# Mamba, token norm, shared expert and routing as one static program, with buffers laid over each other

## The chip, the cores and the metric

The kernel runs on one core of one Trainium2 chip. The metric is the device time in microseconds of one execution, as a median over runs. Smaller is better. All arithmetic is in float32, but for the one-hot tables of the routing (float16).

## What is computed

One layer of a network on an input of 2 sequences of 1024 tokens with 512 features: a Mamba block, then a mixture of experts, each on a layer-normed copy of its input and each with two residuals.

```python
x = L0_attn_x                                   # (2, 1024, 512)
x = x + _L0_attn_ref(_layernorm(x), ...)        # Mamba: D_INNER 1024, 16 states, conv of 4 taps
x = x + _L0_ffn_ref(_layernorm(x), ...)
# in _L0_ffn_ref, T = 2048, H = 512, E = 32 experts of I = 256, K = 4, shared expert of 512:
flat = (x * rsqrt(mean(x**2) + eps) * norm_w).reshape(-1, H)
scores = softmax(flat @ router_w.T)
topk_w, topk_ids = top_k(scores, 4);  topk_w = topk_w / sum(topk_w)
routed = sum over the token's 4 experts of topk_w * (silu(g) * u) @ w2[e],  g, u = split(flat @ w1[e])
shared = (silu(flat @ sg) * (flat @ su)) @ sd
out = x + routed + shared
```

## The kernel before, in words

The program is a sequence of blocks. At the end of a block all engines meet. A block has one stream of instructions for each engine, and semaphores between them. The blocks are `constants`, `mamba`, `tokens`, `routing` and `experts`.

`mamba` is fully unrolled. It goes over 4 segments of 512 tokens (two for each sequence) and in each over 8 channel blocks of 128, so 32 steps g. In a step ScalarE makes the decays (L500), VectorE spreads delta times x over the states (L646) and runs 16 scans (L656), GpSimd multiplies the states by C (L753), and TensorE sums them into `y_ps` (L846) with identity matmuls. Between these sums TensorE does other small pieces, the gap items: the input projection of the next segment ("in"), its delta and B/C projections ("dtr", "bc"), the gate ("z"), the transposes of the normed input ("turn"), and the output projection of the segment before ("out"). They share two PSUM banks (`work`) in turn, by a table `where` that is written out ahead. B and C of a segment go through a DRAM tensor `bcd` and come back replicated to all partitions (`b_rep`, `c_rep`). The last segment's output projection has no step left to hide in: its 4 tiles are the list `closing`. The result x1 is written to DRAM.

`tokens` reads x1 back in 4 groups of 4 tiles of 128 tokens, in loops (`Fori`) on every engine. VectorE and ScalarE make the layer norm and the RMS norm (`norm_steps`), with the weight `norm_w` multiplied in, and the rows `flat` are stored to DRAM for the experts' gathers. For each tile TensorE transposes `flat` (`transposes`, L1091), multiplies by the router, the gate and the up weights (`gate_up`, L1099, L1106), transposes the activation between gate and up of the next tile (`act_transposes`, L1116), and multiplies down (`down`, L1123). VectorE adds the result to `c.base`, which SP stores to the output. The norm of group r+1 stands among the work of group r. The weights, and the first four experts' weights (`w1_ring`, `w2_ring`), are loaded at the start of this block.

`routing` makes from the logits of all 16 tiles the list of tokens for each expert tile: softmax, the four largest, one-hot masks, ranks by matmuls with triangular and one matrices (L1343 to L1345), tile tables, and the list itself from one-hot matmuls (L1355). Nearly all is a chain of small VectorE instructions, each of which waits for the one before (`Chain.settle`).

`experts` goes over the tiles of 128 slots, sorted by expert, two at a time. GpSimd gathers rows of `flat` by an indirect DMA (L1441), TensorE transposes them (L1559), multiplies by w1 (L1573), transposes the activation (L1584), multiplies by w2 (L1591), VectorE scales the rows (L1542), and GpSimd adds them to the output in DRAM by a second indirect DMA (L1456). SP loads the weights of expert e+4 when expert e is done.

## Time and profile before

| what | us |
| --- | --- |
| median of 3 runs | 1881.86 (1879.46 to 1888.6) |
| the profiled execution | 1884.71 |
| its span | 1883.0 |
| TensorE busy | 1613.8 (86%) |
| VectorE busy | 1205.5 (64%) |
| GpSimd busy | 1128.1 (60%) |
| ScalarE busy | 790.8 (42%) |

Times in the profile count from the start of the span. PE is TensorE and PEld its weight loads, DVE is VectorE, ACT ScalarE, POOL GpSimd, SP the engine that issues the plain DMAs. A float32 matmul stands as two records in the trace, so 4 of them are "x8". "128*32" is a matmul whose weights have 32 columns. PEclk is the granted clock of TensorE as a share of 2.4 GHz. In the program's order: Mamba's scan lasts until about 1020, the last output projection until about 1052, tokens until 1277, routing until 1339, and experts to the end.

### The profile page before, as it was taken

Reading aid. Unit: us, or ns where it says so; the run is one execution under the profiler, and the core shown is the slowest. Engines: PE = TensorE matmul, PEld = TensorE weight load, DVE = VectorE, ACT = ScalarE, POOL = GpSimd, SP = SyncE. Lnnn points to the kernel's source line nnn. Section 1 sums busy time; section 2 is a strip of 40 time slices with the busy share of each in tenths; the row PEclk is TensorE's granted clock in tenths of the full one; section 3 lists DMA queues with packets and bytes.
Section 4 is the critical chain, followed back from the end, with each engine's and each line's share of the span. In section 5 each row is a group of like instructions: output and inputs, shape, how many; then the busy total and the mean of one; then the engine's idle time right before and its main releaser. Section 6 shows DMA issues by size and latency. Waiting matters only on the chain. (4 is left out here: it accounts for less than half of the span.)

```text
span 1883.0 us, 18250 instructions
## 1 busy us (share of the span) xinstructions
PE 1613.8 (86%) x4198; PEld 726.3 (39%) x4199; DVE 1205.5 (64%) x1707; ACT 790.8 (42%) x1287; POOL 1128.1 (60%) x695
## 2 busy tenths in 40 slices
PE   5679998999988999898779599992599999999995
PEld 2233433444333444333333254551244444444442
DVE  3599999999999999899994233317532333333331
ACT  4466576665766666566562243410011111111110
POOL 0199899998889988999985111100144444544443
PEclk9889999999999999999999799996699999999998
DMA  3600125101151110410000621210167676676663
GB/s 111 264 18 23 38 65 200 35 33 39 54 209 37 31 36 26 181 43 25 7 17 12 246 85 61 67 39 17 33 150 214 176 198 187 173 196 185 155 145 57
DMA packets 65360, 182.86 MB, mean 97 GB/s; under 512 B 10016, under 2 KB 14368, under 8 KB 56608
## 3 DMA queue, kind: packets, MB, share of 16 engines
q1 hardware_dynamic: 47232, 138.48, 20.8%
q0 software_dynamic: 18080, 43.82, 11.9%
q8 instruction: 20, 0.33, 0.1%
q14 instruction: 28, 0.23, 0.0%
HBM read 147.65 MB, written 34.62 MB: 97 GB/s over the span
## 5 line engine op out<-in xcount | busy, mean ns | idle before, releaser
L753 POOL TENSOR_TENSOR h<-h,c_rep 128x2048 f32<-128x2048 f32 x128 | 579.0, 4527 | 29.9 <-DVE h L656 24.9
L846 PE MATMUL bank<-h,ident 128*128 128x512 f32 x916 | 444.7, 628 | 88.9 <-POOL h L753 68.7
L500 ACT ACTIVATE bank<-delta,a_neg 128x512 f32<-128x512 f32 x512 | 335.8, 681 | 167.2 <-DVE h L656 166.5
L846 PEld LDWEIGHTS bank<-h,ident 128*128 128x128 f32 x916 | 178.3, 199 | 332.6 <-issue 212.9
L656 DVE TENSOR_TENSOR_SCAN h<-bank,state,h 128x512 f32<-128x512 f32 x256 | 305.9, 1259 | 0.5 <-ACT bank L500 0.5
L656 DVE TENSOR_TENSOR_SCAN h<-bank,h 128x512 f32<-128x512 f32 x256 | 290.6, 1199 | 1.4 <-ACT bank L500 1.4
L1573 PE MATMUL h_ps<-w_ring,xT 128*128 x640 | 285.4, 599 | 3.5 <-issue 3.4
L646 DVE TENSOR_TENSOR h<-bank,b_rep 128x2048 f32<-128x2048 f32 (+1 forms) x105 | 227.4, 2184 | 45.1 <-ACT bank L493 31.3
L1524 DVE TENSOR_TENSOR act<-gs,h_ps 128x256 f32<-128x256 f32 x80 | 33.7, 421 | 248.4 <-ACT gs L1497 248.4
L1497 ACT ACTIVATE gs<-h_ps 128x256 f32<-128x256 f32 x80 | 30.7, 384 | 379.6 <-PE h_ps L1573 379.6
L1573 PEld LDWEIGHTS h_ps<-w_ring,xT 128*128 128x128 f32 x640 | 120.8, 191 | 163.3 <-issue 163.3
L1591 PE MATMUL y_ps<-w_ring,aT 128*128 x320 | 149.5, 610 | 11.9 <-ACT aT L1501 11.9
L1456 POOL DMA_INDIRECT out<-y,into x80 | 128.0, 1601 | 30.5 <-issue 26.6
L1440 POOL TENSOR_TENSOR held<-ones 128x1 f32<-128x1 f32 x82 | 22.9, 279 | 191.2 <-DVE which L1534 129.0
L740 POOL TENSOR_TENSOR h<-du,b_rep 128x2048 f32<-128x2048 f32 (+1 forms) x32 | 125.3, 3916 | 12.3 <-PE bank L846 12.3
L806 PE MATMUL bank<-xnT,w_in 128*128 128x512 f32 x256 | 119.8, 615 | 12.2 <-ACT zs L467 10.4
L830 PE MATMUL bank<-xnT,w_res 128*128 128x512 f32 x256 | 119.9, 612 | 0.0
L820 PE MATMUL bank<-w_out,xs 128*128 128x512 f32 x256 | 114.8, 593 | 0.0
L1075 POOL TENSOR_TENSOR base<-x_group,xl_group 128x512 f32 x16 | 22.0, 1406 | 127.8 <-DVE xl_group L1026 127.8
L1441 POOL DMA_INDIRECT xg<-flat,which x82 | 83.3, 1016 | 24.4 <-POOL held L1440 12.3
L1455 POOL TENSOR_TENSOR sent<-ones 128x1 f32<-128x1 f32 x80 | 29.8, 373 | 101.2 <-DMA out<-y,into 88.5
L1591 PEld LDWEIGHTS y_ps<-w_ring,aT 128*128 128x128 f32 x320 | 58.1, 191 | 79.8 <-issue 79.8
(214 smaller groups left out, 1835.9 us busy)
## 6 DMA issues: line engine op xcount, KB each, us to landing
w_ring<-in_w SPq DMA_DIRECT2D x32, 1024.0 KB, 6.2
b_rep<-bcd SPq DMA_DIRECT2D x16, 1024.0 KB, 6.9
c_rep<-bcd SPq DMA_DIRECT2D x16, 1024.0 KB, 4.9
w_ring<-in_w SPq DMA_DIRECT2D x32, 512.0 KB, 8.4
w_in<-in_w_in_x SPq DMA_DIRECT2D x32, 256.0 KB, 2.6
w_res<-in_w_in_res SPq DMA_DIRECT2D x32, 256.0 KB, 2.7
xa<-in_x SPq DMA_DIRECT2D x20, 256.0 KB, 3.0
xb<-in_x SPq DMA_DIRECT2D x16, 256.0 KB, 2.7
```

The lines of the kernel that those rows point to most:

```text
L500: eng.activation(da[j][:], delta[:, g % 2], ACT.Exp, scale=a_neg[:, col:col + 1])\
L646: eng.tensor_tensor(h[:, q, a:b], du_ps[:].unsqueeze(1).to_broadcast([P, b - a, SEG]), b_rep[:, Q * q + a:Q * q + b, :], ALU.mult).then_in ...
L656: eng.tensor_tensor_scan(h[:, q, j, :], da[j][:], h[:, q, j, :], init, ALU.mult, ALU.add)\
L740: eng.tensor_tensor(h[:, q, a:b], du[:].unsqueeze(1).to_broadcast([P, b - a, SEG]), b_rep[:, Q * q + a:Q * q + b, :], ALU.mult).then_inc(S ...
L753: ins = eng.tensor_tensor(h[:, q], h[:, q], c_rep[:, Q * q:Q * q + Q, :], ALU.mult)
L806: ins = eng.matmul(out[:], w_in[:, n % 2, k, :], xnT[:, s % 2, k, :], start=(k == 0), stop=(k == KC - 1))
L820: eng.matmul(out[:], xs[:, s % 2, d, i * P:(i + 1) * P], w_out[:, d, :], start=(d == 0), stop=False)
L830: ins = eng.matmul(out[:], w_res[:, i % 2, k, :], xnT[:, s % 2, k, :], start=(k == 0), stop=(k == KC - 1))
L846: ins = eng.matmul(y_ps[:], c.ident[:], h[:, q, j, :], start=False, stop=(q == NQ - 1 and j == Q - 1))
L1456: eng.indirect_dma_start(out=dram.out_rows, out_offset=bass.IndirectOffsetOnAxis(ap=into[:, u:u + 1], axis=0), in_=y[:, u, :], in_offset=N ...
L1573: ins = eng.matmul(h_ps[i][:], xT[:, i, k, :], c.w1r[:, bass.ds(ring[i], 1), k, :].rearrange("p a n -> p (a n)"), start=(k == 0), stop=(k ...
L1591: ins = eng.matmul(y_ps[i][:], aT[:, i, k, :], c.w2r[:, bass.ds(ring[i], 1), k, :].rearrange("p a n -> p (a n)"), start=(k == 0), stop=(k ...
```

## The change

1. `mamba`, `tokens` and `routing` become one block, `front`, without loops. Its buffers have fixed addresses (`Memory`): `new` takes fresh space, `over` lays a tensor over one that is no longer needed. `c.base` lies over `h`, the shared weights over `xnT` and `w_in`, `flat_T` over `b_rep`, the expert ring over `c_rep` and `w_out`, all tables of the routing over `xs`.
2. The first 12 tiles of x1 are loaded into `c.base` as each quarter of `h` has been summed for the last time. The last 4 tiles never go to DRAM. The norm is made as in Mamba: statistics on VectorE, Ln and Exp on ScalarE, small products on GpSimd, and then one ScalarE instruction a tile for `flat` and one for `base`.
3. `norm_w` is no longer in `flat`. It is multiplied in behind the transposes: `flat_turned` in `front`, `rows_out` in `experts`, both on VectorE.
4. `closing` holds TensorE's whole order from the last output projection to the last down matmul.
5. The routing is cut into nine steps, which VectorE does behind `add(i)` of the shared expert's tiles 0 to 8. TensorE's matmuls for it stand behind `dn(i)`.
6. The B/C projection writes four column groups of 32 partitions, 128 tokens each, in place of one output of 32 x 512. `bcd` is written by four DMAs.
7. The blank rows are stored near the start of Mamba, behind the first `b_rep` and `c_rep` loads, and SP waits for them. Two more small loads stand at the start. The first four gathers are issued at the end of `front`.

```diff
-def mamba(nc, c, dram):
+def front(nc, c, dram):
+        c.base = over("base", "h", [P, TT, DM])
+        w_g, w_u = over("w_sg", "xnT", [P, KC, SH]), over("w_su", "xnT", [P, KC, SH], skip=KC * SH * 4)
+        flT = over("flat_T", "b_rep", [P, TT, KC, P])
...
-        closing = [("out", NSEG - 1, i, half) for i in range(ST) for half in (0, 1)]
+            items = [last(0, 0), last(0, 1), last(1, 0), ft(0), last(1, 1), ft(1), last(2, 0), ft(2), lg(0), last(2, 1),
+                     ft(3), lg(1), last(3, 0), ft(4), lg(2), ft(5), last(3, 1), ft(6), lg(3), ft(7)]
+            for t in range(4, 8):
+                items += [lg(t), ft(t + 4)]
+            items += [lg(t) for t in range(8, 12)]
+            items += [gu(0), ft(12), ft(13), lg(12), ft(14), lg(13), ft(15), lg(14), lg(15)]
+            for i in range(TT):
+                items += ([gu(i + 1)] if i + 1 < TT else []) + [at(i), dn(i), rt(i)]
...
                 def write_bc(s):
                     read(eng, "bc", s, 0)
-                    eng.dma_start(dram.bcd[s], bc[:]).then_inc(S["bcd_written"], 16)
+                    for t in range(ST):
+                        eng.dma_start(dram.bcd[s, :, t * P:(t + 1) * P], bc[2 * NS * t:2 * NS * (t + 1), :])\
+                            .then_inc(S["bcd_written"], 16)
...
+                eng.wait_ge(F["blank_made"], 1)
+                eng.dma_start(dram.flat[T:T + P, :], blank[:]).then_inc(F["blank_stored"], 16)
+                eng.dma_start(dram.out[TT], blank[:, 0:DM]).then_inc(F["blank_stored"], 16)
+                eng.wait_ge(F["blank_stored"], 32)
                 eng.dma_start(w_out[:], dram.w_out).then_inc(S["out_loaded"], 16)
...
+                def load_x1(q):
+                    eng.wait_ge(S["y_summed"], LAST * NQ + q + 1)
+                    for u in range(2):
+                        eng.wait_ge(x1_stored[u], 16 * (q + 1) * ST // 2)
+                    eng.dma_start(c.base[:, q * ST:(q + 1) * ST, :], dram.x1_seg[q]).then_inc(f_loaded[q], 16)
...
+                last_out(0)
+                for t in range(4):
+                    flat_row(t)
+                flat_var(1)
+                flat_root(1)
+                for t in range(4, 8):
+                    flat_row(t)
+                flat_var(2)
+                flat_root(2)
+                residual(NSEG - 1, 2)
+                last_out(1)
+                flat_row(8)
+                residual(NSEG - 1, 3)
+                flat_row(9)
+                last_out(2)
...
+                for i in range(TT):
+                    if i + 1 < TT:
+                        silu_gate(i + 1)
+                    act_turned(i)
+                    if i < 8:
+                        base_row(8 + i)
...
+                for t in range(6, TT):
+                    flat_turned(t)
+                route_scores()
+                mult(0)
+                route_ids()
+                for i in range(TT):
+                    if i + 1 < TT:
+                        mult(i + 1)
+                    add(i)
+                    route(i)
...
+                            for t in range(ST):
+                                ins = eng.matmul(out[2 * NS * t:2 * NS * (t + 1), 0:P], w_xp[:, d, DR:],
+                                                 xs[:, s % 2, d, t * P:(t + 1) * P], start=(d == 0), stop=(d == DC - 1))
...
-                    eng.tensor_scalar(xT[:, i], xT_ps[i][:].rearrange("p (k t) -> p k t", k=KC), 0.0, None, ALU.add)\
-                        .then_inc(S["xT_ready"], 1)
+                    eng.tensor_tensor(xT[:, i], xT_ps[i][:].rearrange("p (k t) -> p k t", k=KC),
+                                      c.norm_f[:].unsqueeze(2).to_broadcast([P, KC, P]), ALU.mult).then_inc(S["xT_ready"], 1)
```

The route steps in order: `route_mask` (tile 0), `route_counts`, `route_places`, `route_tables`, four times `route_hot` for four tiles of tokens, and `route_list` (tile 8). `ft(t)` transposes tile t of `flat`, `lg(t)` multiplies by the router, `gu(i)` by gate and up, `at(i)` transposes the activation, `dn(i)` multiplies down, `rt(i)` is TensorE's part of the routing.

## Rows read from the trace of the kernel before

**Rows 1.** The page, part 1: busy us, share, instructions of each engine.
```profile
PE 1613.8 (86%) x4198; PEld 726.3 (39%) x4199; DVE 1205.5 (64%) x1707; ACT 790.8 (42%) x1287; POOL 1128.1 (60%) x695
```

**Rows 2.** Windows by stage: length, busy us (instructions), PE clock, DMA share, GB/s.
```profile
1020.00:1052.00 32.00, 31.07 (x73) 13.49 (x71) 0.69 (x1) 4.49 (x7) 0.00 (x0) 1.00 0.13 42
1052.00:1080.00 28.00, 6.71 (x20) 4.79 (x21) 10.46 (x19) 7.37 (x16) 6.02 (x5) 0.58 0.91 345
1127.00:1177.00 50.00, 48.74 (x160) 25.05 (x160) 15.37 (x29) 20.55 (x33) 5.50 (x4) 1.00 0.18 63
1277.00:1312.00 35.00, 4.73 (x10) 2.09 (x10) 29.66 (x132) 1.91 (x2) 0.41 (x3) 0.57 0.07 15
1312.00:1339.00 27.00, 8.02 (x64) 4.65 (x64) 25.45 (x136) 0.00 (x0) 0.00 (x0) 0.50 0.00 0
```

**Rows 3.** Chain that ended last, 1335 to 1360: start us, us, what.
```profile
1339.15 0.35 DVE which L1511 x4
...
1345.65 1.13 PE xT_ps L1559 x4
...
1348.83 9.36 PE h_ps L1573 x16
```

**Rows 4.** Timeline, end of Mamba: start, us, what [idle before].
```profile
1020.00 7.03 PE L820 MATMUL bank<-w_out,xs 128*128 128x512 f32 x16
...
1020.20 0.69 DVE L666 TENSOR_TENSOR xs<-bank,zs 128x512 f32<-128x512 f32 x1 [10.19 <-PE bank L846]
...
1050.05 1.02 PE L824 MATMUL bank<-xb,ident 128*128 128x512 f32 x2
```

**Rows 5.** Timeline, start of the tokens stage.
```profile
1062.87 2.48 DVE L1014 BATCH_NORM_STATS2 f_st<-x_group 128x6 f32<-128x512 f32 x4 [41.97 <-DMA x_group<-x]
...
1073.29 1.97 PE L1091 MATMUL tbank<-ident,flat_group 128*128 128x128 f32 x8 [22.22 <-DVE flat_group L1040]
```

**Rows 6.** The page, part 6: issues, KB, median us from issue to landing.
```profile
x_group<-x SPq DMA_DIRECT2D x4, 1024.0 KB, 7.3
```

**Rows 7.** Timeline, opening of Mamba.
```profile
8.09 1.85 SPq L338 DMA_DIRECT2D h<-in_x  x4
...
11.51 0.31 ACT L504 ACTIVATE a_neg<-a_neg 128x128 f32<-128x128 f32 x1 [7.80 <-DMA d_skip<-in_d_skip]
...
16.12 2.93 ACT L432 ACTIVATE h<-h,n_bias,n_scale 128x512 f32<-128x512 f32 x4 [0.92 <-POOL n_bias L720]
...
23.32 0.31 ACT L410 ACTIVATE lnv<-mv,eps_ln 128x4 f32<-128x4 f32 x1
...
25.48 0.21 POOL L720 TENSOR_TENSOR n_bias<-nmean,n_scale 128x4 f32<-128x4 f32 x1
```

**Rows 8.** Timeline, end of the shared expert.
```profile
1259.42 0.97 PE L1099 MATMUL tbank<-w_router,flat_T 128*128 128x32 f32 x8
...
1260.23 3.68 PE L1106 MATMUL tbank<-w_sg,flat_T 128*128 128x512 f32 x8
...
1271.05 0.60 PE L1116 MATMUL tbank<-ident,act_shared 128*128 128x128 f32 x4
...
1272.34 3.70 PE L1123 MATMUL tbank<-w_sd,act_shared_T 128*128 128x512 f32 x8 [0.69 <-ACT act_shared_T L991]
```

**Rows 9.** Timeline, the routing.
```profile
1277.57 0.69 DVE L1200 TENSOR_REDUCE mx<-logits 128x16 f32<-128x512 f32 x1 [0.81 <-PEq L905]
...
1294.52 0.48 DVE L1240 MEMSET hit<- 128x512 f32 x1 [0.17 <-DVE cum L1238]
...
1303.43 0.69 DVE L1284 TENSOR_TENSOR posn<-rank_ps,off 128x512 f32<-128x512 f32 x1
...
1337.17 0.50 PE L1355 MATMUL list_ps<-oh_hi,oh_lo 128*128 128x96 f16 x4 [1.01 <-DVE oh_hi L1331]
```

**Rows 10.** Timeline, B and C projection and first steps of the scan.
```profile
59.61 10.66 PE L813 MATMUL bank<-xs,w_xp 128*32 128x512 f32 x24 [0.56 <-ACT xs L462]
...
109.61 0.83 ACT L432 ACTIVATE xa<-xa,n_bias,n_scale 128x512 f32<-128x512 f32 x1
```

More of the change, by code:

```diff
@@ L46 @@
 RING = 4
+FREE_FROM = 18048
 PASS = 4
@@ new lines, in front, with inside @@
+        fr_scale, fr_bias = new("fr_scale", [P, NSEG, ST]), new("fr_bias", [P, NSEG, ST])
+        c.w1r, c.w2r = over("w1_ring", "c_rep", [P, RING, KC, 2 * FI]), over("w2_ring", "w_out", [P, RING, FC, DM])
+        c.xg = over("xg", "xa", [P, PASS, ROW])
+        c.which, c.held = new("which", [P, PASS], I32), new("held", [P, 1])
+        c.late = mem.home["b_rep"]
+        placed_at = [0]
+        def inside(name, shape, dt=F32):
+            tensor = mem.over(name, "xs", shape, dt, skip=placed_at[0])
+            placed_at[0] += mem.size(shape, dt)
+            assert placed_at[0] <= mem.size([P, 2, DC, SEG], F32)
+            return tensor
@@ new lines, in store_base @@
+                def store_base(i):
+                    read(eng, "dn", 0, i)
+                    eng.dma_start(dram.out[i], c.base[:, i, :]).then_inc(c.base_stored, 16)
+                filled(eng, "z", NSEG - 1, LAST)
+                for dst, src in shared:
+                    eng.dma_start(dst, src).then_inc(F["shared_loaded"], 16)
+                for q in range(NSEG - 1):
+                    load_x1(q)
+                reload_xb(2)
+                store_flat(0)
+                reload_xb(3)
@@ L789, in run @@
                     kind, s, i, half = it
-                    u = where[it[:3]][0]
-                    out = work[u]
-                    if kind not in HALVED or half == 0:
-                        begin(it)
+                    if kind not in UNBANKED:
+                        u = where[it[:3]][0]
+                        out = work[u]
+                        if kind not in HALVED or half == 0:
+                            begin(it)
                     if kind == "turn":
```

1009 lines of the change are left out of this document (491 added, 518 removed).

## The prediction

> **What bounds the kernel now.** I read the busy time by stage first [rows 1, 2]. TensorE is busy 1613.8 of 1883.0 us, so a saving is to be looked for where it is not. The scan (to 1020) and the output projection of the last segment (to 1052) keep it at work, and so does a steady group of four tiles of the shared expert: 48.74 of 50 us busy at a granted clock of 1.00. Three stretches stand out. Between 1052 and 1080 TensorE works 6.71 of 28 us. From 1277 to 1312 it works 4.73 of 35 and from 1312 to 1339 8.02 of 27, while VectorE is busy 29.66 and 25.45: that is the routing, which has the chip to itself, and TensorE's clock falls to the 1.2 GHz level in it (0.57 and 0.50).
>
> The chain that ended last [rows 3] begins for the last part of the run with the token list for the gathers at 1339.15; the first expert matmuls follow at 1348.83 and take 9.36 us for 16 records. After that the chain stays in the experts' stage to the end. So whatever brings that 1348.83 forward shortens the run one for one, as the experts see the same tokens, tiles and order in both kernels.
>
> **The tail of Mamba and the norm.** Before, the last projection runs alone from 1020.00 to 1050.9 [rows 4]: 72 records of 0.43 us, 30.9 us, 7.73 a tile. Then comes a new block: its first statistics wait for the 1 MB load until 1062.87 and its first transposes until 1073.29, with TensorE idle 22.22 us [rows 5]. The change loads the first twelve tiles of x1 over `h` as each quarter of it is summed, in the last 13 us of the scan. Such a 1 MB load lands in 7.3 us [rows 6], the third about 1024. VectorE is free of the scan at 1020.9, after `gate(LAST)` [rows 4]; four statistics are 2.48 [rows 5], so the three groups' are there at about 1024, 1027 and 1030.
>
> ScalarE then runs a chain of scales for each group, 2.4 us from `lnv` to `n_bias`, and a row costs it 0.73 [rows 7]. In the written order it does: scales 0 (to 1026.2), `last_out(0)` when tile 0 is summed (1027.9 to 1028.5), rows 0 to 3 (1031.4), scales 1 (1033.7), rows 4 to 7 (1036.7), scales 2 (1039.1), a residual and only then `last_out(1)`, at 1040.4. TensorE, which may start half tile 1, `ft(0)` and the other half without a pause, is done at 1035.9, and its next item, `ft(1)`, takes the bank of output tile 1. This is a new wait of 4.5 us, and everything on TensorE stands behind it. The same pattern costs 0.9 us behind `last_out(2)` and 0.9 behind `last_out(3)`; short waits for VectorE's `flat_turned` add some 1.2. After a pause of this kind I add 2 us for records at the lower clock: the first eight after the 22.22 us pause took 1.97 [rows 5]. In all 9.5 us of stalls (bounds 2 and 20).
>
> **The shared expert.** A tile is 24 weight records of 0.43, 10.3 us, the router's 0.81 (1259.42 to 1260.23), and two sets of four transposes, 0.60 with the tail and 0.44 charged [rows 8]. Before, the transposes of the activation are hidden between gate and up. The new order is `gu(i+1), at(i), dn(i), rt(i)`: `dn(i)` stands right behind `at(i)`, and that wait is seen in the trace only for a last tile: transposes at 1271.05, first down record at 1272.34 behind ScalarE's copy [rows 8]. 1.29 us, and 0.05 more because ScalarE has `silu_gate` first. So 16 × 1.34 = 21.4 us.
>
> **The routing.** VectorE's 61 us, from 1277.57 to just before the new block's 1339.15 [rows 3, 9], are cut into nine steps after `add(i)`. The longest is `route_counts` (1294.52 to 1303.43, 8.9 us with its wait for TensorE); places, tables and four steps of hot rows share the 33.7 us from there to 1337.17. A tile of the new order is 11.6 us on TensorE. VectorE's own two operations in it are some 1.4 (15.37 us a group before, which then held the norm too [rows 2]), so 8.9 + 1.4 fits, and a step delays only `mult(i+2)`, which is wanted a tile later. What hides the routing is thus the matmuls of tiles 0 to 8; without that cover its 61 us are back. What TensorE does for it now stands in its own queue at full price: ranks, counts and tile tables about 2.2 us, and 64 one-hot matmuls; four took 0.50 at half clock [rows 9], so 6 us with their dispatch. Sum 8.2. Its operands are there: `route_counts` ends in the tile before `rt(2)`.
>
> **The sum to the first expert matmul.** From 1020.0: output 30.9, 16 × 0.44 + 16 × 0.81 for `ft` and `lg` = 20.0, weights 16 × 10.3 = 164.8, activation transposes with their wait 21.4, routing 8.2, stalls 9.5. Together 254.8, so the last down matmul ends at 1274.8 where it ended at 1275.8 (1272.34 and eight records). From there the block's end cost 1.8 us, to 1277.57. The four gathers are by then long landed (list ready behind tile 8), so of the experts' start only transposes, their copies and the issue remain: from 1345.65 to 1348.83, 3.2 us [rows 3], with 0.2 for a first start. First expert matmul at 1280.0 instead of 1348.83: **−68.8 us**.
>
> **Smaller parts.** The first 16 expert records took 9.36 us, against 6.9 (16 × 0.43) at full clock. Now TensorE comes from work, but with some 5 us nearly idle: I take −1 (bounds 0 and −2.5). The copy of `xT` becomes a multiply with a broadcast operand: 512 elements from PSUM, on VectorE under the 3.4 us of `y`, nothing; if it were uncovered, less than 0.1 a tile. At the opening two more small loads stand before the second x tiles: ScalarE waited for the last of the small ones until 11.51 [rows 7], and two issues of 0.46 (four took 1.85 just behind) make it +1.0. The blank rows are written behind the `b_rep` and `c_rep` loads and SP waits for them, with `w_out`, two `w_in`, `w_dt(2)` and the third `xa` behind it. The first of these wanted is `xa`, at 109.61 [rows 10]; the b/c loads are issued from about 65, and at the 345 GB/s of the loads behind 1052 [rows 2] their 8.4 MB take 24 us and the 3.5 MB behind them 10, an estimate of 100. So 9 us of margin hide it, and without them the step would wait for the rest. Four writes of `bcd` for one: three more issues of 0.46, at the opening under the `dtr` matmuls, at the other boundaries under the scan of the step.
>
> The B and C projection turns from 16 records of 128x512 (6.9 of the 10.66 us behind 59.61 are such records and `dtr`'s [rows 10]) into 64 records of 128 columns in four column groups. The nearest rows price a short record at 0.10 to 0.11: 64 × 0.11 = 7.0 us, +0.2. If four ran beside each other it would be 1.8; the second half of it, 3.4 us before and 0.9 then, is on the opening's chain, so 2.6 us less there. No row shows either; I take 0, bounds −2.6 and +0.5, and nothing for the three later boundaries, where VectorE is the full engine.
>
> The Trainium skill ("TensorEngine Tiling (Array Packing)", Theoretical Speedup) lets four column tiles of 32 run at once, up to four times as fast, and its Instruction Overhead section puts a floor of about 60 cycles under each matmul. By that rule the opening would be up to 2.6 us shorter, and the forecast about 1810; no row here shows column tiles side by side.
>
> Total −68.8 − 1 + 1.0 = −68.8. The profiled execution took 1884.71 us for a span of 1883.0, so 1815.9; it lies 2.9 above the median of the runs, and by the median I say **1813 us**.
>
> **Rivals.** (a) As forecast, 1799 to 1829: 0.71. (b) The routing steps do hold TensorE: VectorE is in order, and one step that lasts over about 15 us, or a wait in it for a `rt` that comes a tile later, stops `mult`. If a third of the 61 us shows, 1833. For it: `route_counts` and `route_list` both wait for TensorE. Against: the arithmetic of 10.3 in 11.6. 0.12. (c) The experts' stage gives some back: another phase of the weight loads against them can cost 15: 1828. For it: the chain of waits holds gathers and scatters besides matmuls. Against: the same order and the same tiles. 0.08. (d) The other side: TensorE stays at 1.2 GHz through the projection, norm and shared expert, since these have more short pauses than before. Their 222 us of matmuls would double, 2035; it decides from 31% of them on. For it: the clock falls in the routing and at 1052 [rows 2]. Against: 1.00 in the projection and in the shared expert, with 1.3 us of pause in 50 [rows 2], and the new pauses of 0.9 a tile stand between 10.3 us of work. 0.04. (e) The change doesn't do what it says, and the routing stands exposed: 61 more, less the 8.2 counted already, 1866, and 1881 with (c) on top. It needs every step to be late at once, as by a wrong order of the queues: 0.05, of which 0.03 within 0.5%.
>
> **How the numbers follow.** Bounds of (a): stalls −7.5 and +10.5, the column groups −2.6, the clock −1.5 and +1, and the waits of `at` ±4. Range for 8 in 10: 1797 to 1838, which takes in (b) and (c) and leaves out (d), (e) and the ends. A change of 0.5%, 9 us, is about what can be told. Faster 0.93, same 0.03, slower 0.04.
>
> **What would show it.** Transposes of `flat` between halves of the last projection from 1031 on, with a pause of 4 to 5 us before `ft(1)`; `gu(1)` at 1085; 12.1 us a tile to dn(8), 11.6 behind; the token list ready near 1195; the first expert matmul at 1280 and from there 534 us to the end of the span, within 3. Wrong if the pause is over 15 us, if VectorE's `mult` releases `at`, or if the experts' stage has another length.

## The result and the profile after

The changed kernel took 1809.49 us (median of 4 runs, 1808.02 to 1814.91) against 1884.36 for the kernel before on the same chip: ratio 0.961, 95% interval 0.959 to 0.963. The forecast was 1813, between 1797 and 1838. The profiled execution took 1814.91 for a span of 1813.2; for it I had 1815.9. The forecast's saving was 68.8 us: the two profiled executions differ by 69.8, the two medians by 74.9, since the profiled execution of the changed kernel is the slowest of its four.

Part 1 of the page of the changed kernel, which answers to [rows 1] (busy us, share, instructions):

```profile
PE 1596.5 (88%) x4390; PEld 726.5 (40%) x4391; DVE 1187.3 (65%) x1675; ACT 736.4 (41%) x1231; POOL 1110.7 (61%) x704
```

Its windows, which answer to [rows 2] (stretch; its length, then busy us and instructions of TensorE, its weight loads, VectorE, ScalarE and GpSimd, TensorE's clock, DMA share, GB/s). They are the projection with part of the norm, what follows, four tiles of the shared expert, and the two stretches that held the routing:

```profile
1020.00:1052.00 32.00, 28.79 (x79) 13.53 (x77) 12.17 (x30) 12.78 (x30) 3.03 (x18) 0.95 0.48 177
1052.00:1080.00 28.00, 26.73 (x150) 19.26 (x151) 7.79 (x15) 12.31 (x21) 1.36 (x9) 0.94 0.62 226
...
1136.00:1186.00 50.00, 46.69 (x148) 21.79 (x149) 26.07 (x122) 7.54 (x13) 0.00 (x0) 1.00 0.06 22
1277.00:1312.00 35.00, 30.16 (x88) 14.52 (x88) 10.30 (x27) 2.86 (x8) 10.23 (x14) 0.95 0.30 73
1312.00:1339.00 27.00, 26.43 (x79) 12.72 (x78) 8.58 (x25) 3.24 (x9) 13.92 (x18) 1.00 0.74 184
```

In the second stretch TensorE is busy 26.73 us instead of 6.71. In the tiles VectorE is busy 26.07 of 50 us instead of 15.37, the routing being in there, and TensorE still works 46.69. The last two stretches are experts now.

TensorE's timeline over the same part (start, us, what, idle before it and who ended that):

```profile
1021.59 7.03 PE L1327 MATMUL bank<-w_out,xs 128*128 128x512 f32 x16
...
1040.75 1.11 PE L1346 MATMUL bank<-ident,flat_rows 128*128 128x128 f32 x4 [3.10 <-ACT base L743]
1041.66 4.62 PE L1327 MATMUL bank<-w_out,xs 128*128 128x512 f32 x8
...
1052.59 0.66 PE L1346 MATMUL bank<-ident,flat_rows 128*128 128x128 f32 x4 [0.69 <-ACT base L743]
...
1075.21 4.98 PE L1362 MATMUL bank<-w_sg,flat_T 128*128 128x512 f32 x8
...
1089.50 3.68 PE L1362 MATMUL bank<-w_sg,flat_T 128*128 128x512 f32 x8
...
1273.58 3.67 PE L1372 MATMUL bank<-w_sd,act_shared_T 128*128 128x512 f32 x8 [0.78 <-ACT act_shared_T L784]
1279.38 1.07 PE L1599 MATMUL xT_ps<-ident,xg 128*128 128x128 f32 x8 [2.13 <-DVEq L1550]
1282.59 8.82 PE L1613 MATMUL h_ps<-w_ring,xT 128*128 x16 [2.15 <-issue]
```

The pause ahead of `ft(1)` (3.10 us, the line of 1040.75) is there, ended by ScalarE's copy of output tile 1, which is line L743, and the first expert matmul starts at 1282.59 where it started at 1348.83. TensorE's groups over the shared expert name the wait of the down projection (busy us, mean ns of one, idle us before and what ended it), and VectorE's and GpSimd's timeline says when the list was ready:

```profile
L1372 PE MATMUL bank<-w_sd,act_shared_T 128*128 128x512 f32 x128 | 58.7, 601 | 13.2 <-ACT act_shared_T L784 13.2
```

```profile
1202.15 0.34 DVE L1116 CAST which<-slot_token 128x1 int32<-128x1 f32 x4
...
1203.38 1.18 POOL L1275 DMA_INDIRECT xg<-flat,which  x1 [0.62 <-POOL held L1274]
```

### The profile page after: what moved, and what is told of

Its sections match the earlier page's. It is cut to its first block and busy times, and to the rows that moved or that the text cites. A ratio compares the mean times of both kernels' runs of the same rounds, so it can differ in the third digit from the quotient of the medians.

```text
span 1813.2 us, 18146 instructions
## 1 busy us (share of the span) xinstructions
PE 1596.5 (88%) x4390; PEld 726.5 (40%) x4391; DVE 1187.3 (65%) x1675; ACT 736.4 (41%) x1231; POOL 1110.7 (61%) x704
## 5 line engine op out<-in xcount | busy, mean ns | idle before, releaser
L1402 PE MATMUL bank<-h,ident 128*128 128x512 f32 x916 | 452.6, 638 | 95.6 <-POOL h L1217 74.7
L1305 PE MATMUL bank<-xnT,w_in 128*128 128x512 f32 x256 | 118.5, 609 | 12.5 <-ACT zs L628 10.7
L1484 POOL DMA_INDIRECT xg<-flat,which x78 | 79.3, 1016 | 22.6 <-POOL held L1483 12.0
```

The lines of the kernel that those rows point to most:

```text
L1305: ins = eng.matmul(out[:], w_in[:, n % 2, k, :], xnT[:, s % 2, k, :], start=(k == 0), stop=(k == KC - 1))
L1402: ins = eng.matmul(y_ps[:], c.ident[:], h[:, q, j, :], start=False, stop=(q == NQ - 1 and j == Q - 1))
```

## The experiments

All are edits of the changed kernel. They were run on three chips, on each beside the kernel before (medians 1882.68, 1886.38 and 1884.71 us), so ratios are compared and not times. Whole times of one program differ by some microseconds between executions as well, so beside the ratio each has a **mark**: the time in its trace from the first record of the last output projection to the first expert matmul. It is 1348.83 − 1020.00 = 328.8 before and 1282.59 − 1021.59 = 261.0 after. The stage behind it, to the end of the span, is 534.2 and 530.6. The last column is the time in that stage in which TensorE waits for a gather to land. All three columns are in us, from one profile each.

| kernel | ratio to before (95%) | mark | stage behind | waits for gathers in it |
|---|---|---|---|---|
| before | 1 | 328.8 | 534.2 | 11.7 |
| changed | 0.961 (0.959 to 0.963) | 261.0 | 530.6 | 9.6 |
| changed again | 0.9615 (0.960 to 0.963) | 261.0 | 532.5 | 10.2 |
| routing behind | 0.992 (0.989 to 0.995) | 316.6 | 528.4 | 7.4 |
| B/C whole | 0.963 (0.960 to 0.965) | 261.3 | 526.7 | 7.7 |
| copy early | 0.958 (0.956 to 0.961) | 257.5 | 530.5 | 9.1 |
| transposes between | 0.955 (0.953 to 0.958) | 246.6 | 535.5 | 9.9 |
| gathers behind | 0.966 (0.964 to 0.968) | 266.4 | 534.4 | 9.7 |
| norm behind | 0.968 (0.966 to 0.970) | 273.2 | 528.3 | 5.8 |
| norm behind, x1 late | 0.975 (0.972 to 0.978) | 285.2 | 539.2 | 11.7 |
| norm behind, fed | 0.968 (0.966 to 0.970) | 268.2 | 531.5 | 9.0 |
| routing in one lump | 0.9875 (0.986 to 0.989) | 308.5 | 533.2 | 8.2 |
| combined | 0.9515 (0.949 to 0.954) | 241.3 | 535.8 | 10.2 |
| combined, gu(0) forward | 0.951 (0.950 to 0.953) | 242.8 | 528.0 | 7.7 |

The mark itself can differ by 1.3 us between executions. The gate matmuls of tile 0 stand behind 11 us of small matmuls; they took 4.98 to 5.31 us in six profiles and 3.68, at full clock, in the profiles of "transposes between" and "routing in one lump", whose TensorE order up to there is that of the changed kernel.

**Is the tiles' cover the gain?** The nine steps of the routing, from the mask on, behind the last add (in SP's queue the stores of the shared expert's tiles all come ahead of the store of the weights, too):

```diff
                     add(i)
-                    route(i)
+                for i in range(9):
+                    route(i)
...
-                items += ([gu(i + 1)] if i + 1 < TT else []) + [at(i), dn(i), rt(i)]
-            return items
+                items += ([gu(i + 1)] if i + 1 < TT else []) + [at(i), dn(i)]
+            return items + [rt(i) for i in range(9)]
```

> The nine steps of the routing (mask to list) are all taken on VectorE behind the last add, and their matmuls and the store of the weights behind the last down projection; scores and ids stay ahead of the tiles. Theory (the gain at the first experts is the cover of the tiles over VectorE's steps): they are exposed again. In the kernel before, the steps from the mask on took some 46 us up to 1339.15; TensorE's queue is lighter by 4 in the tiles, the gathers are exposed for 6.5, and the first expert records run at the lower clock for 2. First expert matmul 50 us later (1283 to 1333), time about 1859, ratio to the kernel before 0.987. Rival 1 (the routing steps hold up TensorE in the tiles, so that much of the gain was lost there): the tiles get shorter than the 11.8 us of the last ones, and the loss is under 40. Rival 2 (the gain came from the norm or from elsewhere): loss under 15 us.

Measured: 1867.71 us, mark 316.56, 55.6 later. From the first projection record to the last down projection it is 5.5 us shorter (246.44 instead of 251.99), from there to the experts 61.1 longer. The tiles of the changed kernel lost no more than TensorE's own routing matmuls (four tiles with 16 of the one-hot ones take 12.55 instead of 11.80, and the ranks and tables 2.5), so the steps on VectorE held nothing up; rival 1 falls, and rival 2 too. I was 5.6 us low, and VectorE's timeline says why:

```profile
1267.90 2.49 DVE L1004 TENSOR_TENSOR oh<-iota,idx 128x512 f32<-128x512 f32 x4
...
1319.92 0.34 DVE L1114 CAST which<-slot_token 128x1 int32<-128x1 f32 x4
```

From the mask to the list the nine steps take 52.0 us, and took 53.0 in the kernel before (1286.19 to 1339.15), not the 46 of what I expected here and in the next experiment. The list is ready 52.9 us behind the last down matmul; less the 5.5 by which the tiles are shorter, that is 47.4 us for the steps. From the list to the first expert matmul it is 13.8 us, where 5.6 follow the last down matmul in the changed kernel. These other 8.2 of the 55.6 us are the gathers and the start of the experts' block.

**Does the cutting matter, or only the place?** All nine steps behind the add of tile 3, with their matmuls in one piece behind `dn(3)` (and on SP the store of the weights behind the store of tile 3):

```diff
                     add(i)
-                    route(i)
+                    if i == 3:
+                        for n in range(9):
+                            route(n)
...
-                items += ([gu(i + 1)] if i + 1 < TT else []) + [at(i), dn(i), rt(i)]
+                items += ([gu(i + 1)] if i + 1 < TT else []) + [at(i), dn(i)]
+                items += [rt(n) for n in range(9)] if i == 3 else []
```

> All nine routing steps stand in one piece on VectorE behind the add of tile 3, and their matmuls in one piece on TensorE behind the down projection of tile 3. Theory (the tiles cover the routing only because it is cut into steps shorter than a tile): TensorE stands for the whole of the steps, some 46 us less the 4 that it works in them itself; output to first expert matmul 303 to 308, against 261.0 cut and 316.6 with the routing behind all tiles, where the gathers and the cold start are exposed too. Rival (VectorE's order beside the shared expert costs less, since TensorE may run on into other work): under 285.

Measured: 1861.49 us, mark 308.5, half a microsecond over what was expected. TensorE's timeline there:

```profile
1131.06 3.67 PE L1375 MATMUL bank<-w_sd,act_shared_T 128*128 128x512 f32 x8 [0.83 <-ACT act_shared_T L785]
1144.24 2.08 PE L1379 MATMUL bank<-mask,tri 128*128 128x512 f32 x2 [9.52 <-DVE hit L1017]
...
1152.11 0.48 PE L1384 MATMUL bank<-ident,same 128*1 128x96 f32 x2 [3.81 <-DVE etile L1049]
...
1163.59 0.50 PE L1391 MATMUL bank<-oh_hi,oh_lo 128*128 128x96 f16 x4 [10.68 <-DVE oh_hi L1106]
1165.10 0.50 PE L1391 MATMUL bank<-oh_hi,oh_lo 128*128 128x96 f16 x4 [1.01 <-DVE oh_hi L1106]
```

The same work in the middle of the shared expert, not behind it, costs 47.5 us of the 55.6, and 1.3 more without the full clock at the gate of tile 0. TensorE takes its items in order and stands for each step, 9.52, 3.81 and 10.68 us and then 1.01 for every four one-hot matmuls, and in 1137 to 1187 its granted clock is 0.50. That is the steps' whole 47 us: the twelve tiles of the shared expert still to come hide nothing of one lump, and the 8 us that it saves are the gathers and the start, which are early again. So what hides the routing is the cutting into steps that fit in a tile, together with the matmul of each step placed one tile behind it. The two were not parted: no run has the steps in a lump on VectorE only, or on TensorE only.

**The gathers.** The first four, moved from the end of `front` to the start of the experts' block:

```diff
-                for u in range(PASS):
-                    eng.wait_ge(F["which_ready"], u + 1)
-                    eng.wait_ge(c.held_done, u + 1)
-                    eng.tensor_tensor(c.held[:], c.ones[:, 0:1], c.ones[:, 0:1], ALU.mult).then_inc(c.held_done, 1)
-                    eng.indirect_dma_start(out=c.xg[:, u, :], out_offset=None, in_=dram.flat,
...
+                for u in range(PASS):
+                    eng.wait_ge(c.held_done, u + 1)
+                    eng.tensor_tensor(c.held[:], c.ones[:, 0:1], c.ones[:, 0:1], ALU.mult).then_inc(c.held_done, 1)
+                    eng.indirect_dma_start(out=c.xg[:, u, :], out_offset=None, in_=dram.flat,
...
                 for u in (0, 1):
                     gather(1, u)
```

> The first four gathers are issued by GpSimd at the start of the experts' block instead of behind tile 8 of the shared expert; all else is as changed. From the start of the last output projection to the first expert matmul the changed kernel takes 261.0 us. Theory (the early gathers are a term of the gain, as the list is ready 75 us before the experts): the 6.5 us from the list to the first transposes come back, less some 1 us of the block's start that they share, and the first records run colder: 267 to 269, time 6 to 9 us more. Rival (a gather is hidden by the start of the block, or its early landing only brings a later wait forward): under 2 us.

Measured: 1820.54 us, mark 266.4, 5.4 later; a little under what I expected (267 to 269), and well over the rival. The experts' start there:

```profile
1269.38 3.67 PE L1365 MATMUL bank<-w_sd,act_shared_T 128*128 128x512 f32 x8 [0.78 <-ACT act_shared_T L784]
1279.23 1.11 PE L1598 MATMUL xT_ps<-ident,xg 128*128 128x128 f32 x4 [6.18 <-DMA xg<-flat,which]
1280.78 1.12 PE L1598 MATMUL xT_ps<-ident,xg 128*128 128x128 f32 x4 [0.44 <-DMA xg<-flat,which]
```

The wait for the gather takes the place of the block's own 2.13 us. By the ratio it is 9 us more; what is over 5.4 lies in parts that differ between executions (below).

**The B and C projection.** Put back to matmuls of 512 columns into 32 rows, alone:

```diff
-                            for t in range(ST):
-                                ins = eng.matmul(out[2 * NS * t:2 * NS * (t + 1), 0:P], w_xp[:, d, DR:],
-                                                 xs[:, s % 2, d, t * P:(t + 1) * P], start=(d == 0), stop=(d == DC - 1))
+                            ins = eng.matmul(out[0:2 * NS, :], w_xp[:, d, DR:], xs[:, s % 2, d, :], start=(d == 0), stop=(d == DC - 1))
...
```

> The B and C projection alone is put back as 8 matmuls of 128x512 into 32 rows, with one write of bcd; all else is as changed. Theory (the column groups save 1.6 us on the opening's chain, but TensorE then pauses 3.1 us and its clock falls, so dtr and what follows give it back; the later boundaries are VectorE's): first spread on VectorE about 1 us later, the end of the span within 1 us, ratio within 0.001 of the changed kernel's 0.961. Rival 1 (column groups are worth 2.6 us and more at the opening, and the same again at each of three boundaries): 3 to 8 us slower. Rival 2 (their short records and cold clock cost): 2 to 4 us faster.

Measured: 1813.38 us, ratio 0.963 where the changed kernel has 0.961 and 0.9615; within the intervals they can't be told apart, and so the time alone doesn't exclude the lower end of rival 1 either. TensorE in the opening, first in the changed kernel, then put back:

```profile
54.09 1.08 PE L1312 MATMUL bank<-xs,w_xp 128*32 128x128 f32 x32 [0.17 <-DVE xs L866]
...
58.28 1.94 PE L1312 MATMUL bank<-xs,w_xp 128*32 128x128 f32 x32 [3.11 <-ACT xs L623]
...
60.15 9.07 PE L1320 MATMUL bank<-xs,w_xp 128*128 128x512 f32 x16
```

```profile
55.19 3.62 PE L1309 MATMUL bank<-xs,w_xp 128*32 128x512 f32 x8 [0.17 <-DVE xs L864]
59.37 3.59 PE L1309 MATMUL bank<-xs,w_xp 128*32 128x512 f32 x8 [0.56 <-ACT xs L621]
62.89 7.13 PE L1316 MATMUL bank<-xs,w_xp 128*128 128x512 f32 x16
```

Four column groups do run beside each other: 32 records of 128 columns in 1.08 us, where 8 of 512 took 3.62. But TensorE is then idle for 3.11 us instead of 0.56, and the next two pieces run at the lower clock for some of their length: 1.94 and 9.07 instead of 1.08 and 7.13. VectorE's idle time before the first spread, 19.46 us with whole matmuls in two profiles, is 18.3 to 18.6 in seven profiles with column groups and 19.7 to 19.9 in five. So at the opening 1 us is won in some executions and 0.4 lost in others, by when the clock comes back.

The same seven and five part again later. From the first spread to the start of the last output projection it is 939.5 to 940.1 us in the seven, 942.7 to 944.4 in the five, and 941.7 and 941.9 with whole matmuls. So the projection starts at 1015.7 to 1017.4 in the seven, at 1019.9 to 1021.6 in the five (the changed kernel's first profile is one of them), and at 1019.9 and 1020.0 with whole matmuls. By these starts the column groups would be worth 2.5 to 4.3 us in some executions and nothing, or 1.6 us lost, in others; with two profiles of whole matmuls that is no more than an estimate. What parts the two sets the second time, from about 300 us on, isn't shown.

**ScalarE's order.** The copy of output tile 1 ahead of the scales of group 2:

```diff
                 for t in range(4, 8):
                     flat_row(t)
+                last_out(1)
                 flat_var(2)
                 flat_root(2)
                 residual(NSEG - 1, 2)
-                last_out(1)
                 flat_row(8)
```

> On ScalarE alone, the copy of output tile 1 goes ahead of the scales of group 2 instead of behind them and a residual. Theory (TensorE's pause of 3.10 us ahead of ft(1) is ScalarE's order, and the half tile behind it runs at the lower clock for 1 us more): the pause shrinks to under 1, the first expert matmul comes 3 to 4 us earlier, ratio 0.959. Rival (the pause only moves: ft(2), rows 8 to 11 or the group of residuals are late instead, since ScalarE has 1 us of slack in 30): less than 1 us.

Measured: 1805.23 us, ratio 0.958, mark 257.5, 3.5 earlier, as expected:

```profile
1033.10 0.65 PE L1346 MATMUL bank<-ident,flat_rows 128*128 128x128 f32 x4 [1.02 <-ACT base L743]
1033.59 3.60 PE L1327 MATMUL bank<-w_out,xs 128*128 128x512 f32 x8
```

The wait is 1.02 instead of 3.10, and the half tile behind it takes 3.60 instead of 4.62. No later wait grew.

**The place of the transposes.** The activation's, back between gate and up of the next tile, and their copy ahead of the next silu:

```diff
-                items += ([gu(i + 1)] if i + 1 < TT else []) + [at(i), dn(i), rt(i)]
+                items += [("ga", 0, i + 1, 0), at(i), ("up", 0, i + 1, 0)] if i + 1 < TT else [at(i)]
+                items += [dn(i), rt(i)]
...
                 for i in range(TT):
+                    act_turned(i)
                     if i + 1 < TT:
                         silu_gate(i + 1)
-                    act_turned(i)
...
```

> The transposes of the activation are put back between the gate and the up matmuls of the next tile (TensorE's order is gate, transposes, up, down, routing), and on ScalarE the copy of them goes ahead of the next gate's silu. Theory (in the changed kernel each down projection waits 0.83 to 0.99 us for that copy, 13.2 us over the 16 tiles): 15 of 16 waits go, the first expert matmul comes 12 to 14 us earlier, time 1796 to 1798, ratio 0.954. Rival (the routing steps on VectorE then release the transposes, which are wanted 3.4 us earlier in the tile than now): in the tiles of the long steps, 1, 2 and 3, a wait for VectorE takes its place, up to 9 us in all, so 4 to 8 us earlier only.

Measured: 1800.43 us, ratio 0.955, mark 246.6, 14.4 earlier where 12 to 14 were expected. TensorE's whole list of waits from the gate of tile 0 to the block's end, without those for its own queue (us in total, times, longest):

```profile
PE bank L1370 <- DVE act_shared L962: 2.8, 1, 2.8
PE bank L1375 <- ACT act_shared_T L785: 0.8, 1, 0.8
PE bank L1353 <- DVE flat_T L955: 0.4, 1, 0.4
```

The down projections wait no more, but for the last. The rival's wait is there once, in tile 0, not in the tiles of the long steps: `mult(0)` stands behind `route_scores` on VectorE, and the transposes, wanted earlier now, wait 2.8 us for it. A tile takes 10.74 instead of 11.80, 15.9 us over fifteen, and `gu(0)` happened to run at full clock, 1.3 us; less 2.8 that is 14.4. So the edit itself is worth some 13.

**The overlap of the norm with the projection.** The projection whole on TensorE, its copies ahead of the scales and rows on ScalarE, the reload of the last `xb` ahead of the stores on SP, x1 still loaded early:

```diff
-            items = [last(0, 0), last(0, 1), last(1, 0), ft(0), last(1, 1), ft(1), last(2, 0), ft(2), lg(0), last(2, 1),
...
+            items = [last(i, half) for i in range(ST) for half in (0, 1)]
+            items += [ft(0), ft(1), ft(2), lg(0), ft(3), lg(1), ft(4), lg(2), ft(5), ft(6), lg(3), ft(7)]
...
```

> The overlap of the norm with the last output projection alone is undone: on TensorE the whole projection comes first, on ScalarE its four copies come ahead of the scales and rows; the twelve tiles of x1 are still loaded as the scan frees their place, and VectorE's statistics are early. Theory (the overlap itself is worth about nothing here, as the stalls behind ScalarE and the clock eat it; what was won on the norm are the early loads): output to first expert matmul 261.0 in the changed kernel, here 258 to 263. Rival (the overlap is worth the norm's own 20 us of TensorE and ScalarE's chain): 270 or more.

Measured: 1823.86 us, ratio 0.968, mark 273.2: my theory was wrong by 12 us, and the mark is what the rival had. TensorE's timeline:

```profile
1045.71 1.02 PE L1329 MATMUL bank<-xb,ident 128*128 128x512 f32 x2
1050.61 2.55 PE L1344 MATMUL bank<-ident,flat_rows 128*128 128x128 f32 x12 [3.87 <-ACT flat_rows L766]
...
1072.54 1.09 PE L1344 MATMUL bank<-ident,flat_rows 128*128 128x128 f32 x4
1073.42 6.87 PE L1350 MATMUL bank<-w_router,flat_T 128*128 128x32 f32 x32
1080.11 6.38 PE L1360 MATMUL bank<-w_sg,flat_T 128*128 128x512 f32 x8
1086.33 3.60 PE L1360 MATMUL bank<-w_su,flat_T 128*128 128x512 f32 x8
```

It pauses only 3.87 us and then has no further wait up to the gate of tile 0, but the clock does not return in 30 us of small matmuls: a window from 1046 to 1086 gives 0.57, where the changed kernel has 0.96 from 1045 to 1086. Four transposes and a router group take 2.46 us instead of 1.28. It comes back in the gate matmuls of tile 0. Twelve such pairs take 29.5 us, where 12 × 1.28 would be 15.4, and the gate 2.8 more than at full clock: 16.9 us at the lower clock against 2.8 in the changed kernel. That is more than the 12.2, since the changed kernel waits and loses some 2 us more in other places.

**Is it the clock or ScalarE's chain?** The order of the last kernel, against which this cut is shown, with two whole tiles of gate and up in it (they are taken out further down):

```diff
-            items += [ft(0), ft(1), ft(2), lg(0), ft(3), lg(1), ft(4), lg(2), ft(5), ft(6), lg(3), ft(7)]
+            items += [ft(0), ft(1), gu(0), ft(2), lg(0), ft(3), lg(1), ft(4), lg(2), ft(5), gu(1), ft(6), lg(3), ft(7)]
...
```

> The kernel with the norm behind the projection took 273.2 us from output to first expert matmul, 12.2 more than the changed kernel, and I had expected nothing. Its transposes and router matmuls ran at 1.2 GHz from the 3.87 us pause on: a tile of them took 2.46 us where it takes 1.28 in the changed kernel. Here the same order gets two whole tiles of gate and up matmuls in it, gu(0) behind ft(1) and gu(1) behind ft(5). Theory (the overlap's worth is the clock: small matmuls alone do not bring it back, full ones do): most router groups take 0.81 again, and the 12 us come back nearly whole: 261 to 264. Rival (the overlap's worth is ScalarE's chain of scales and rows, which is exposed once the projection is gone): 270 or more, with waits for flat_rows between the tiles.

Measured: 1823.63 us, ratio 0.968, mark 268.2. By the mark it lies between theory and rival:

```profile
1054.84 1.94 PE L1344 MATMUL bank<-ident,flat_rows 128*128 128x128 f32 x8 [3.88 <-ACT flat_rows L766]
1056.80 5.66 PE L1360 MATMUL bank<-w_sg,flat_T 128*128 128x512 f32 x8
1062.30 3.60 PE L1360 MATMUL bank<-w_su,flat_T 128*128 128x512 f32 x8
...
1066.17 0.98 PE L1350 MATMUL bank<-w_router,flat_T 128*128 128x32 f32 x8
...
1099.81 1.09 PE L1365 MATMUL bank<-ident,act_shared 128*128 128x128 f32 x4 [6.34 <-DVE act_shared L959]
1101.67 5.41 PE L1370 MATMUL bank<-w_sd,act_shared_T 128*128 128x512 f32 x8 [0.78 <-ACT act_shared_T L784]
```

The clock part holds: behind `gu(0)` all small matmuls run at full clock (0.91 over 1046 to 1086 instead of 0.57), and no wait for `flat_rows` stands between them, so it is not ScalarE's chain that the rival of the last experiment had. But a new wait came at the end: with `gu(0)` and `gu(1)` used up early, nothing covers `route_scores` on VectorE, behind which `mult(0)` stands, 6.34 us, and 2.2 at the lower clock behind it (1.09 and 5.41 instead of 0.60 and 3.67). Without those 8.5 us the mark would be 259.7, an estimate; the time itself did not get better.

**The early loads of x1.** As the kernel with the norm behind, against which the cut is shown, and `load_x1` waits for the last output tile:

```diff
+                reload_xb(2)
+                reload_xb(3)
+                filled(eng, "out", NSEG - 1, ST - 1)
                 for q in range(NSEG - 1):
                     load_x1(q)
-                reload_xb(2)
-                reload_xb(3)
                 store_flat(0)
```

> As the kernel with the norm behind the projection, and also the loads of x1 wait for the last output tile, as in the kernel before. Theory (early loads are what was won on the norm): the first load's 7.3 us and four statistics of 2.5 us come onto the path, 9 to 11 us more than the kernel with the norm behind the projection. Rival (the loads would be hidden by ScalarE's copies and the clock): less than 4 us more.

Measured: 1840.17 us, ratio 0.975, mark 285.2, 11.9 more than with early loads; 9 to 11 were expected. The wait ahead of the first transposes is 12.11 us instead of 3.87, one more of 1.44 follows, and `gu(1)` too starts at the lower clock (5.38 instead of 3.68).

**Two better versions.** The early copy and the transposes between, with two router groups ahead of the flat transposes that wait 0.69 us for an output copy:

```diff
             items = [last(0, 0), last(0, 1), last(1, 0), ft(0), last(1, 1), ft(1), last(2, 0), ft(2), lg(0), last(2, 1),
-                     ft(3), lg(1), last(3, 0), ft(4), lg(2), ft(5), last(3, 1), ft(6), lg(3), ft(7)]
+                     lg(1), ft(3), last(3, 0), ft(4), lg(2), ft(5), last(3, 1), lg(3), ft(6), ft(7)]
```

> A version that might beat both: transposes of the activation between gate and up, the copy of output tile 1 ahead of the scales of group 2, and two of the router's groups put between an output tile and the flat transposes that wait for its copy (twice 0.69 us). Theory (the three savings lie on one path and add up): output to first expert matmul 246.6 (transposes between) less 3.5 (early copy) less 1.4 = 242 to 243, ratio to the kernel before 0.950 to 0.953. Rival (the experts' stage or the clock gives some back): the mark is reached but the time is not below that of the kernel with the transposes between, 1800 us, ratio 0.955.

Measured: 1793.98 us, ratio 0.9515, mark 241.3, where 242 to 243 were expected: the three add up, to some 1% under the changed kernel. A second version moves gate and up of tile 0 in between the norm's small matmuls:

```diff
             for t in range(4, 8):
-                items += [lg(t), ft(t + 4)]
-            items += [lg(t) for t in range(8, 12)]
-            items += [gu(0), ft(12), ft(13), lg(12), ft(14), lg(13), ft(15), lg(14), lg(15)]
+                items += [lg(t), ft(t + 4)] + ([("ga", 0, 0, 0)] if t == 5 else [])
+            items += [lg(8), lg(9), ("up", 0, 0, 0), lg(10), lg(11)]
+            items += [ft(12), ft(13), lg(12), ft(14), lg(13), ft(15), lg(14), lg(15)]
```

> The combined version with the gate and up matmuls of tile 0 moved forward, each between groups of the norm's small matmuls. Theory (in the combined version the first eight records of gu(0) run at the lower clock for 1.4 us, after 10 us of small matmuls): output to first expert matmul 241.25 less 1.4 = 239.9, ratio within 0.001 of the combined version's. Rival (the tile moved forward makes ft(12) or the first multiply late): no gain, or up to 3 us more.

Measured: 1792.54 us, ratio 0.951, mark 242.8: no gain, and my premise was wrong. In the profile of the combined version the first eight records of `gu(0)` took 3.68 us, at full clock; the lower clock there belongs to some executions only, as said of the mark. TensorE in this one:

```profile
1080.95 3.68 PE L1364 MATMUL bank<-w_sg,flat_T 128*128 128x512 f32 x8
1087.46 0.63 PE L1370 MATMUL bank<-ident,act_shared 128*128 128x128 f32 x4 [2.83 <-DVE act_shared L962]
1087.92 5.29 PE L1364 MATMUL bank<-w_su,flat_T 128*128 128x512 f32 x8
```

The 2.83 us behind `route_scores` are in the combined version too, but there the up matmuls behind them took 3.60, here 5.29, and that 1.7 is about the 1.5 between the two marks. Taking `mult(0)` ahead of `route_scores` would be the next thing to do; it wasn't tried.

**The same program again.**

> The changed kernel itself once more, to see what differs between executions of one program. In nine profiles the part up to the last output projection, the same code in nearly all, ended between 1015.7 and 1021.6, and the experts' stage took 526.7 to 539.2 us. Theory (both differences are between executions, and TensorE's waits for the gathers go with the second): output to first expert matmul 261.0 within 0.5, the other two anywhere in these ranges, and the stage longer where TensorE waits longer for gathers (5.8 us of waits at 528.3, 11.7 at 539.2). Rival (they belong to each kernel's timing): 1021.6 and 530.6 within 1.

Measured: 1811.92 us, mark 261.02, the projection at 1017.04 instead of 1021.59 and a stage of 532.5 with 10.2 us of waits for gathers. The mark repeats within 0.1; the other two do not. The start of the projection is here that of the seven profiles of above. Of the seven longest stages in the table (532.5 to 539.2) six have waits of 9.7 to 11.7 and one of 8.2; the four shortest (526.7 to 528.4) have 5.8 to 7.7. The stage's length goes with these waits, though they differ by 5.9 us and the stage by 12.5, so they are at most half of it. Why gathers land later in one execution than in another isn't settled by these runs, nor is the other half.

## Why the prediction was right

**The sum to the last down matmul.** From the start of the projection I had 254.8 us; 255.4 were taken (1277.0 − 1021.59, the last record's end by 8 of 0.43). By its terms: stalls 7.7 for 9.5 (3.10, 0.69, 0.69 and 0.44 of waits, and 1.4 twice at the lower clock), the routing on TensorE 5.5 for 8.2, the activation's transposes with their wait 11.80 − 10.3 = 1.5 a tile, 24.0 for 21.4. `ft` and `lg` took 16 × 1.28 = 20.5 for 20.0. With output and weights as forecast that makes 253.4; 2.0 I can't assign. The errors are 1 to 3 us and of both signs, so that the sum is within 1 us is in part luck. Of the routing's 2.7 too much, the one-hot matmuls are 3: 4 × 0.75 = 3.0 us for my 6. Two of my signs did not agree with my own sum: its terms put `gu(1)` 67.3 us behind the projection's start and not 65, and it came at 67.9; and they give 12.5 us a tile up to dn(8) and not 12.1, and it is 12.4.

**The start of the experts.** 5.6 us from there, for 5.2 forecast. The gathers had landed; their term is 5.4 us where they are put behind. The list was ready at 1202.15, 7 us later than said, which costs nothing.

**What hides the routing.** This step carries most of the forecast, and it was shown from two sides: behind the tiles the routing costs 55.6 us, and in the tiles but in one lump 47.5. Rival (b) is excluded for the changed kernel: no tile waits for VectorE. Its longest step is the mask, from 1102.19 to 1110.92, 8.7 us in a tile of some 12, and not `route_counts`. I had the 61 us of VectorE's routing all in the nine steps. They are 52; the scores and ids, some 9 us (1089.70 to 1098.9), stand ahead of them at the first tiles. In the changed kernel nothing waits for these, but the scores, ahead of `mult(0)`, are the wait of 2.8 us that came up when the transposes moved.

**The norm.** The new wait ahead of `ft(1)` was forecast at 4.5 us with 2 of clock and was 3.10 with 1.4; the place and the cause were right, as the early copy shows. The size was off by ScalarE's scales of group 2:

```profile
1038.05 0.28 ACT L748 ACTIVATE f_lnv<-f_mv,eps_ln 128x4 f32<-128x4 f32 x1
...
1039.42 0.80 ACT L600 ACTIVATE xb<-xb,r_bias,r_scale 128x512 f32<-128x512 f32 x1
1040.12 0.57 ACT L743 ACTIVATE base<-bank 128x512 f32<-128x512 f32 x1
```

I had charged them 2.4 us, up to GpSimd's last product, but the residual that stands behind them doesn't use that product, and ScalarE was free after 1.37. The larger miss is another. I had priced the overlap by its stalls alone, and what it buys I had not seen: with the norm behind, the mark is 12.2 us longer by the clock, and 11.9 more with late loads. The sum was right because I had taken every record of the closing part at full clock, for which the only reason given was the 1.00 in the projection and the tiles of before; that it would hold among so many small matmuls was luck as much as reasoning. Rival (d), the lower clock, didn't come in this order (0.99 from the projection's start to the first expert matmul), but the kernel with the norm behind shows that an order near it meets it in part.

**The opening.** The +1.0 for two more small loads did not appear: ScalarE had the last of them at 11.36 against 11.51. My 0 for the column groups came out right within what the ratios can tell, though not for its reason. The Trainium skill ("TensorEngine Tiling (Array Packing)", Theoretical Speedup) has four column tiles of 32 at up to four times the speed, and the trace agrees: 1.08 us for 3.62, 3.4 times. What it would do to the time did not follow, because TensorE waits for ScalarE right behind and then runs slower. The first spread was at 77.21, where it was at 78.27 before; with column groups it is at 76.1 to 78.0 over twelve profiles, with whole matmuls in the changed kernel at 78.02.

**The experts' stage.** It took 530.6 us for 534 forecast within 3, so by the letter of my own sign it has another length. But with 526.7 to 539.2 over fourteen profiles that bound was too narrow, and the 3.6 us between the kernel before and the first profile of the changed one are not a gain that can be ascribed to the change. The 15 us of rival (c) had no row behind it; the 12.5 between the shortest and the longest stage is what these profiles have. The projection's start, 1015.7 to 1021.6, moves the whole time as well. The multiply with a broadcast operand in the copy of `xT` took 0.69 us, where the copy before took 0.70.

## What to carry to other kernels

Routing, or any long chain on another engine, was hidden by matmuls when it was cut into steps shorter than a tile and TensorE took each step's matmul a tile later (no run tells how much each of the two does); in one piece in the middle of the tiles it costs as many microseconds as its steps take (47.5 us here, and 55.6 behind everything, where the gathers are late too). Four transposes and a router group took 1.28 us among large ones and 2.46 alone behind a pause, so the worth of interleaving a norm with a projection is partly the clock, and moving the large ones about can uncover another engine's chain elsewhere. Where a down projection waits 0.8 us a tile for a copy, putting those transposes one operation earlier gave some 13 us for an edit of a few lines: the table of waits shows such a thing as one row with many small pieces.

## What the hardware showed unexpectedly

- After a 3.87 us pause TensorE stayed at the 1.2 GHz level through 30 us of transposes and router matmuls without another wait (granted clock 0.57), and came back in the eight records of the next 128x512 matmuls. With such matmuls put in behind the first transposes, the same small ones ran at 2.4 GHz.
- A pause of 3.11 us in place of 0.56 took back what column groups had won: the sixteen records behind it took 7.7 to 8.2 us in some executions of the same code and 9.1 to 9.3 in others, for 7.1 without the pause.
- The twelve profiles with column groups fall into the same two sets at the opening (18.3 to 18.6 us of VectorE's idle time, or 19.7 to 19.9) and over the 940 us behind it (939.5 to 940.1, or 942.7 to 944.4).
- TensorE's waits for the same gathers in the same code were 5.8 to 11.7 us in all, and the stage's length varied by 12.5 us beside them.
